# A drain carries the count of summed unit pairs in a graph kernel's second neighbour sum

## What is computed

```python
x = _layernorm(x + _L0_gnn_ref(x, ...))        # first layer: messages, segment_sum, matmuls
# second layer
feat_in  = h @ W_in.T + b_in
feat_out = h @ W_out.T + b_out
a_in  = _seg_mean(feat_in[src], dst, N)        # mean over a node's edges, one direction
a_out = _seg_mean(feat_out[dst], src, N)       # and the other
a = jnp.concatenate((a_in, a_out), axis=1)
h = _gru_cell(a, h, w_ih, w_hh, b_ih, b_hh)
x = _layernorm(x + h)
```

## Time and profile before

| | |
|---|---|
| median of 3 runs | 8651.19 us (8642.64 to 8704.52) |
| the profiled execution's own time | 8592.66 us |
| its span | 8591.0 us |
| PE / DVE / ACT / POOL busy | 57% / 37% / 20% / 61% |
| neighbour sums | about 3458 to 8394 us of the span |

### The profile page before, as it was taken

The page is one execution under the profiler, slowest core; times in us unless marked ns, Lnnn a source line. Parts: engine busy times, 40 slices in busy tenths (PEclk is TensorE's granted clock), DMA queues, the critical chain, the costliest instruction groups (busy, mean ns, idle before and its releaser), DMA issues.

```text
span 8591.0 us, 115667 instructions
## 1 busy us (share of the span) xinstructions
PE 4860.7 (57%) x27117; PEld 4156.9 (48%) x27117; DVE 3136.4 (37%) x6639; ACT 1682.3 (20%) x4659; POOL 5270.2 (61%) x6008
## 2 busy tenths in 40 slices
PE   5888888888888899122232322323344444444337
PEld 4777777777777799122222322323233333333333
DVE  7555555555555567111111311112111111111128
ACT  2222222222223366100000000000111111111006
POOL 2556555555655676656666666665666666666654
PEclk7666667676767799566666666666666666666668
DMA  3222223222222598222222122221222222222225
GB/s 107 91 90 97 93 90 96 92 93 93 95 91 93 170 310 276 67 43 46 46 46 46 42 46 46 47 47 37 55 63 62 64 62 63 62 64 62 51 60 159
DMA packets 903626, 722.39 MB, mean 84 GB/s; under 512 B 601771, under 2 KB 703782, under 8 KB 902874
## 3 DMA queue, kind: packets, MB, share of 16 engines
q1 hardware_dynamic: 628082, 338.08, 14.6%
q0 software_dynamic: 161968, 341.31, 13.7%
q10 hardware_dynamic: 113469, 41.94, 1.9%
HBM read 556.95 MB, written 170.31 MB: 85 GB/s over the span
## 4 chain that ended last, share of the span: by engine, by line
another core or an unknown queue 34%; issue 11%; PE 9%; ACTq 4%; DVE 3%; ACT 2%; DVEq 2%; DMA 1%; POOL 0%; SPq 0%; POOLq 0%
PE bank L1966 5%; PE bank L2015 2%; DVE acc_b L1656 1%; ACTq L418 1%; DVEq L418 1%; DMA arena<-blktab 1%; ACTq L1035 1%; DVE acc_a L396 0%; ACT arena L1052 0%; ACTq L1066 0%; ACT acc_a L1014 0%; ACTq L1038 0%; DVE arena L1650 0%; PE bank L2071 0%
## 5 line engine op out<-in xcount | busy, mean ns | idle before, releaser
L821 POOL DMA_INDIRECT arena<-x1d,edge x3322 | 3142.5, 946 | 1741.9 <-issue 968.8
L2015 PE MATMUL bank<-arena 128*128 x8256 | 1438.7, 346 | 2245.4 <-DVE acc_b L1656 1575.9
L2015 PEld LDWEIGHTS bank<-arena 128*128 128x128 f32 x8256 | 1369.7, 257 | 2345.2 <-issue 2326.9
L762 POOL DMA_INDIRECT msgs<-arena x1664 | 1646.3, 989 | 1249.3 <-DVE arena L1436 774.5
L1650 DVE TENSOR_TENSOR arena<-bank,arena 128x1024 f32<-128x1024 f32 x516 | 631.2, 1224 | 3893.1 <-remote 3289.5
L1052 ACT ACTIVATE arena<-edge,arena 128x4 f32 x1032 | 224.7, 286 | 3159.7 <-issue 2951.4
L1916 PE MATMUL bank<-w2s,acc_b 128*128 128x128 f32 x3328 | 744.7, 392 | 20.1 <-issue 19.7
L1916 PEld LDWEIGHTS bank<-w2s,acc_b 128*128 128x128 f32 x3328 | 631.0, 282 | 160.6 <-issue 160.6
L1899 PE MATMUL bank<-arena 128*128 (+1 forms) x3328 | 662.8, 352 | 76.4 <-issue 72.8
L1899 PEld LDWEIGHTS bank<-arena 128*128 128x128 f32 x3328 | 585.5, 258 | 95.1 <-issue 92.6
L1401 DVE TENSOR_TENSOR_SCAN acc_b<-arena,acc_b 128x512 f32<-128x512 bf16 x415 | 531.7, 1281 | 7.4
(11 more groups left out here) (320 smaller groups left out, 5334.4 us busy)
## 6 DMA issues: line engine op xcount, KB each, us to landing
arena<-msgs SPq DMA_DIRECT2D x512, 272.0 KB, 4.9
arena<-rows SPq DMA_DIRECT2D x208, 512.0 KB
arena<-x1d,edge POOLq DMA_INDIRECT x3322
msgs<-arena POOLq DMA_INDIRECT x1664
pred<-arena ACTq DMA_DIRECT2D x98, 256.0 KB
arena<-pred SPq DMA_DIRECT2D x12, 1792.0 KB, 8.5
arena<-xwin SPq DMA_DIRECT2D x208, 64.0 KB
arena<-in_edge_attr_dram SPq DMA_DIRECT2D x207, 32.0 KB
```

Of the source, the lines that this page charges most:

```text
L762: pool.indirect_dma_start(msgs, bass.IndirectOffsetOnAxis(ap=pos[:, b, j:j + 1], axis=0), mrow[:, b, j, :], None).then_inc(scattered[b], 16)
L821: pool.indirect_dma_start(grow_t[:, sl, 0:D], None, x1d, bass.IndirectOffsetOnAxis(ap=edge2[:, odd * RING + sl, 1:2].bitcast(i32), axis=0) ...
L2015: last = mm(sum_at(q, u), oh1[:, q % 2, u * UT + k, :], rows[:, k * CW:(k + 1) * CW], start=(k == 0), stop=(k == UT - 1))
```

## The change

```diff
@@ -2013,7 +2013,7 @@
                         rows = grow[:, bass.ds(rows_at[q * UG + u], UT * CW)]
                         for k in range(UT):
                             last = mm(sum_at(q, u), oh1[:, q % 2, u * UT + k, :], rows[:, k * CW:(k + 1) * CW], start=(k == 0), stop=(k == UT - 1))
-                    last.then_inc(s["sum1_ready"], 1)
+                    pe.drain().then_inc(s["sum1_ready"], 1)
                     if block is not None and q == 0:
                         pre_turned(*block)
                     if block is not None and q == 1:
```

## The result

| | before | changed |
|---|---|---|
| median (lowest to highest, runs) | 8653.43 us (8642.64 to 8704.52, 4) | 8931.60 us (8921.12 to 8966.53, 4) |
| the profiled execution's own time | 8592.66 us | 8938.87 us |

The changed kernel takes 1.0317 of the time, 95% interval 1.0266 to 1.0367: slower by 278 us, where 453 us of gain were forecast. The time is within 1% of the 9020 us of the rival *"Held, and TensorE's queue stands behind the drain: slower"*, whose loss of 370 us was a third too large.

The account below looks back on a forecast made before the run. GpSimd's gathers were taken as the bound, stalled because TensorE's count is held while they stream. -393 - 60 + 0 = -453 us from 8651 gave 8198 us (-5.2%), range 7960 to 8780; faster 0.51.

Parts of the forecast that it names:

- Held, and TensorE's queue stands behind the drain: slower: Rival: the drain blocks the next pair, rounds serve two pairs, not three; +370 us, 9020 (in part 8740); chance 0.19.
- The loop of 174 rounds: Both halves' sums: GpSimd fills the ring, stops, the count gets out, about 3.0 pairs follow; 4.4 us lost per round.
- the floor of 4152 us: Both halves' gathers: 3322 at 1.25 us each cannot take less; they took 4936 us.
- held back while GpSimd streams: In the sums: TensorE's count is held during GpSimd's indirect DMAs and comes out when the stream runs dry.
- the part on what is removed: Increment taken off the product: if only the increment is held, counting another way frees the loop.
- the -393: GpSimd's line 619 waits freed in half one (372.8 us) and after 7986 (50.0), less issue: 393 us gained.
- the -60: From 6126 to 7986, drains behind held `x_t` and `pre_lin`: a fifth of 280 us gained; ends 0 and 280.
- below 50 us: Sign of being right: GpSimd's waits on line 619 in half one fall under this.
- The drain is held like the product: no change: Rival: the drain's count comes at the same time as the product's; 8651 us, 8630 to 8700; chance 0.30.
- the bound of 8480: Slow end of the forecast case: only half one's 343 us freed and nothing of the rest.
- The cost of the drains: 516 added TensorE drains: taken as 0, hidden under GpSimd; up to 607 us if all lay open.
- as long as before, with the drain's record stretching over them (the product ends late): Sign of a wrong mechanism: "remote" waits stay as long, covered by the drain's record.

Follow-up runs that it names:

- drain_first_half: Kernel before, with the count on TensorE's drain in the first half's 258 pairs and on the last product in the second's: 8743.06 us, 1.0121 (chip 8).
- self_wait_2: Kernel before, with no drain: count on the last product, and TensorE's own program waits for that count: 8913.00 us, 1.0290 (chip 4).
- extra_drain_2: Kernel before, count left on the last product, plus a drain without increment behind it: 8912.75 us, 1.0281 (chip 4).
- pause_16_drain: Kernel before, with GpSimd stopping after every 16 gathers until they land and draining, and the count on TensorE's drain: 8667.40 us, 1.0092 (chip 2).
- extra_drain: Kernel before, count left on the last product, plus a drain without increment behind it, on chip 9: 7278.84 us, 1.0004.

## Why the prediction was wrong

**What bounds the kernel: right in the main.** The loop of 174 rounds, the count that mostly comes 2 to 3 us after GpSimd's last gather, and the floor of 4152 us all stand; chip 9, which holds no count, runs at that floor (4166 us). So does "indirect DMAs": with direct ones the hold is gone (VectorE's longest wait for a product is 4.7 us). But "held back while GpSimd streams" says too much. Nearly half of the completions are prompt (225 of 516 drains within 0.1 us), the first pair after a stop among them.

**The step that failed** is the first of the part on what is removed: "If the product itself is over at its recorded end, and only its increment is held, then counting in another way frees the loop." On these chips this does not hold, whether the condition is false or only nothing in TensorE's reach learns of the product's end in time. A drain that carries no increment ends up to 40.7 us after its matmuls, so the -393 and the -60 had nothing to come from. In half one the waits on line 619 rose from 372.8 us (87) to 511.3 (120), where "below 50 us" was to be seen; in all they rose to 1113.3. The evidence on which the step leant was the recorded end of a product, and the profile says of that end that it is modelled. On chip 9 the model is right to 0.05 us, which is no warrant for a chip on which drains end 40 us later. The one row that tested it pointed the other way: matmuls stood stuck behind a held product. I read it as a matter of `pre_lin` alone, and took the 12 matmuls that still issued as a sign that the array was through, which they do not show.

**What TensorE loses: the rival, over-sized.** It named the mechanism and the point from which it decides ("if the drain ends only with the stream, not at the recorded end of the products"), which the drain's records show. Its sum was 84 more rounds at 4.4 us, +370. Measured: 62 more at 1113.3 / 236 = 4.7 us, the waits together +345, own time +346. The rounds served 2.2 pairs and not 2, and 225 drains were prompt; the rival took it that in every round exactly one pair fewer gets through. The medians differ by 278 only, because the profiled execution of before lay 60.8 us under the median of its four runs and that of the changed kernel 7.3 us over its own. With 0.19 the rival had too small a chance.

**"The drain is held like the product: no change": half right.** The argument against it, that SyncE's and VectorE's increments "pass promptly during gathers", leant on a row in which GpSimd was standing still, so it did not show that. Held alike the drain is: 43.1 us is the longest in the products' half and in the drains' half of `drain_first_half`. But it does not follow that nothing changes, as the drain also stops what stands behind it. `self_wait_2` shows that part by itself, with no drain.

**A drain behind a held `x_t`: not the cause.** The term of 60 us out of 280 supposed that only from 6126 to 7986 drains would be held. They are held in the first half too, which has no `x_t`: in `drain_first_half` 128 of its 258 drains end more than 3 us late, and it loses 98 us.

**A small slip in the sum.** Half one alone gives 372.8 - 26.1 = 347 us and not 343; the bound of 8480 stays.

**The cost of the drains: right under cover, open otherwise.** Taken at 0 under GpSimd, with ends 0 and 607: on chip 9 under gathers it is 0 (7278.84 against 7276.17), laid open 289 us, 0.56 each, about half of the 1177 ns of the only drain of before. On the slow chips it was not measured apart from the hold.

**Signs.** Waits "as long as before, with the drain's record stretching over them (the product ends late)" was the sign given for a wrong mechanism, and it is what the profile after shows: 2032.3 us in 225 waits in half one, which now have the drain's name, where 1786.3 us in 104 were "remote".

## What to carry to other kernels

A long wait by "remote" for a TensorE count does not say that the increment alone is late. The test is a drain that raises nothing: compare its end with the recorded end of the matmuls before it, not its length. When a completion is late for reasons outside the program, a drain or a wait for it in the engine's own program takes away look-ahead, here 0.8 of the 3.0 pairs of a round, so leave the increment on the product. Whether more depth in the loop would help was not tried. And before a loss is looked for in the program, see whether another chip of the same kind has it.

## What the runs showed of the hardware

- On every chip used but one many of TensorE's completions came late while GpSimd streamed indexed DMAs 1.25 us apart. Of the 516 drains of the changed kernel 225 ended within 0.1 us of the recorded end of their matmuls and 228 more than 3 us after it, up to 40.0 us; 178 of those 228 ended when GpSimd had stood still for more than 1.5 us. The other chips: 230 of 516 on chip 4 (`extra_drain_2`), 128 of 258 on chip 8 (`drain_first_half`) and 235 of 516 on chip 2 (`pause_16_drain`) more than 3 us after it. Increments and drains were late alike (VectorE waited at most 43.1 us for either in `drain_first_half`), and a TensorE that waits for its own count lost as much as one with a drain (8913.00 and 8912.75 us on chip 4). VectorE's were not seen to be: in the trace of before TensorE's waits before line 2015 ended with an instruction of VectorE 149 times and without an owner 4 times (28.1 us).
- On chip 9 the kernel before took 7276 us instead of some 8650. There, in `extra_drain`, all 516 drains ended within 0.05 us of the recorded end. Why the chips differ was not found, and nor was what inside the indexed DMA, or in the reporting of completions, does it.
- GpSimd's direct DMAs of the same size (0.54 us each) and indexed ones 3.3 us apart did not cause it: VectorE's longest wait for a product was 4.7 us with the first, and with the second 492 of its waits before the one-hots ended with the product and none without an owner.
- A TensorE drain's record in the sums was at least 1.02 us long and began 1.0 to 3.9 us before the recorded end of its pair's matmuls (changed kernel); each drain cost 0.56 us where nothing covered it (chip 9, no gathers).
